# Cross-attention in plain float32: one product per term in the last attention block of a four-block decoder

## The reference, cut to what matters

```python
def _L3_xattn_ref(hidden_states, cross_attention_states, attention_mask, q_proj_w, k_proj_w, v_proj_w, o_proj_w, q_norm_w, k_norm_w):
    q = (hidden_states @ q_proj_w.T)...            # 32 heads of 128
    k = (cross_attention_states @ k_proj_w.T)...   # 8 kv heads, 64 keys per batch
    v = (cross_attention_states @ v_proj_w.T)...
    q = rmsnorm(q, q_norm_w); k = rmsnorm(k, k_norm_w)
    scores = einsum('bhqd,bhkd->bhqk', q, k) / sqrt(128) + attention_mask
    attn = softmax(scores)
    out = einsum('bhqk,bhkd->bhqd', attn, v)...
    return out @ o_proj_w.T
...
x = x + tanh(g_xattn[3]) * _L3_xattn_ref(_layernorm(x), ctx_4096, mask, ...)
```

## Time and profile before

| | us |
|---|---|
| median of 3 runs | 1882.77 |
| lowest, highest | 1882.39, 1884.41 |
| the profiled execution | 1874.59 |
| its span, first to last instruction | 1872.9 |

### The profile page before, as it was taken

How to read it: one execution, slowest core, us unless ns; L and a number is a source line. 1 busy time by engine, 2 the same in 40 slices (tenths; PEclk the granted TensorE clock), 3 DMA queues, 4 the chain that set the end, 5 groups by cost and what they waited for, 6 DMA issues and landing times.

```text
span 1872.9 us, 18291 instructions
## 1 busy us (share of the span) xinstructions
PE 1460.5 (78%) x6556; PEld 1020.8 (55%) x6556; DVE 1213.1 (65%) x1816; ACT 611.7 (33%) x912; POOL 348.9 (19%) x330
## 2 busy tenths in 40 slices
PE   7878778778746678578878888779999999997104
PEld 5545454445324545365746666557777777776101
DVE  4887888788885677542354444646666665667777
ACT  3544444444432233210121221134444344443003
POOL 1122132122213700010000000112212222123600
PEclk9998998989878799789569999989999999998556
DMA  5675776665572000002010112101101111000001
GB/s 193 156 181 137 143 178 150 160 141 138 117 136 99 34 11 1 0 23 68 0 34 17 46 38 77 48 9 57 57 23 39 53 57 57 1 1 1 0 0 45
DMA packets 37183, 127.69 MB, mean 68 GB/s; under 512 B 4288, under 2 KB 10304, under 8 KB 30896
## 3 DMA queue, kind: packets, MB, share of 16 engines
q1 hardware_dynamic: 26224, 83.38, 13.1%
q0 software_dynamic: 10880, 43.26, 13.0%
HBM read 72.63 MB, written 10.75 MB: 45 GB/s over the span
## 4 chain that ended last, share of the span: by engine, by line
PE 58%; DVE 20%; issue 10%; DVEq 5%; ACT 3%; POOL 1%; POOLq 1%; DMA 1%; SPq 0%
PE PS L151 10%; PE PS L153 9%; PE PS L152 9%; PE PS L492 6%; PE PS L467 4%; PE PS L825 3%; PE PS L861 3%; DVE AR L610 3%; DVE AR L2082 2%; DVEq L320 2%; DVE AR L631 2%; PE PS L451 2%; DVE AR L2076 2%; DVE AR L2080 1%; PE PS L847 1%
## 5 line engine op out<-in xcount | busy, mean ns | idle before, releaser
L492 PE MATMUL PS<-R,PT 128*128 128x512 f32 x256 | 158.0, 775 | 130.3 <-DVE X L646 130.3
L492 PEld LDWEIGHTS PS<-R,PT 128*128 128x128 f32 x256 | 61.5, 252 | 215.8 <-issue 215.8
L152 PE MATMUL PS<-R16r 128*128 128x512 f32 (+1 forms) x328 | 122.9, 375 | 0.0
L153 PE MATMUL PS<-R16r 128*128 128x512 f32 (+1 forms) x312 | 121.2, 388 | 0.0
L467 PE MATMUL PS<-R,HT 128*128 128x256 f32 x512 | 115.9, 379 | 0.0
L400 POOL DMA_DIRECT2D AR<-AR x40 | 49.6, 1240 | 307.7 <-DMA AR<-AR 239.4
L467 PEld LDWEIGHTS PS<-R,HT 128*128 128x128 f32 x512 | 94.8, 190 | 11.6
L151 PE MATMUL PS<-R16r,HTr 128*128 128x512 f32 (+1 forms) x224 | 91.3, 408 | 6.1 <-DVE X L1218 4.6
L151 PE MATMUL PS<-HTr,R16r 128*128 128x512 f32 (+1 forms) x240 | 90.4, 377 | 3.1 <-DVE R16r L193 1.6
L610 DVE SCALAR_TENSOR_TENSOR AR<-OT,AR 128x2112 f32<-128x2112 bf16 x32 | 75.5, 2359 | 21.8 <-ACT OT L555 19.4
L153 PE MATMUL PS<-HTr,R16r 128*128 128x512 f32 (+1 forms) x240 | 88.3, 368 | 0.0
(11 more groups left out here) (284 smaller groups left out, 3702.8 us busy)
## 6 DMA issues: line engine op xcount, KB each, us to landing
AR<-AR POOLq DMA_DIRECT2D x40, 1056.0 KB, 8.2
OR<-in_wo SPq DMA_DIRECT2D x12, 1024.0 KB, 5.0
dequantised<-AR SPq DMA_DIRECT2D x8, 1056.0 KB, 4.5
WR<-in_w0q SPq DMA_DIRECT2D x8, 1024.0 KB, 5.9
AR<-in_w3q SPq DMA_DIRECT2D x8, 1024.0 KB, 4.9
WR<-dequantised SPq DMA_DIRECT2D x22, 256.0 KB, 2.8
AR<-in_nf SPq DMA_DIRECT2D x4, 1056.0 KB, 6.0
nf_in<-in_nf SPq DMA_DIRECT2D x4, 1056.0 KB, 5.9
```

Of the source, the lines that this page charges most:

```text
L152: nc.tensor.matmul(out, ah, bl, start=False, stop=False)
L153: return nc.tensor.matmul(out, al, bh, start=False, stop=last_)
L492: i = nc.tensor.matmul(bank(5 + tt), PT[:, at:at + P], vo[:, pr, b, :], start=pr == 0, stop=pr == 1)
```

## The change

The queries and outputs of x3 are computed with one plain float32 product in the place of mm3, and nothing makes high and low parts for them any more. `VO`, `PT` and `HT0` are the float32 views of the same places. The rounds of `piece`, the folded pieces and the turned probabilities are released by ACT's copy alone. Query weights are loaded straight into one of two places that the product reads. `turn_p(u)`'s copies alternate between two halves of `PT`.

```diff
+        PLAIN = (0, 6, 7)
@@ dve_norm
             def low(t):
-                if n == 0:
+                if n in PLAIN:
                     return
@@ pe_norm
-                if t >= 2:
+                if t >= 2 and n in PLAIN:
+                    pe.wait_ge(hi_ready, T * n + t - 1)
+                elif t >= 2:
                     pe.wait_ge(lo_ready, T * (n - 1) + t - 1)
@@ act_norm
-                nc.scalar.copy((HT0 if n in (0, 7) else HTh)[:, :, t * P:(t + 1) * P],
+                nc.scalar.copy((HT0 if n in PLAIN else HTh)[:, :, t * P:(t + 1) * P],
@@ places
+        VO = R16[:, 4096:8192].rearrange("p (r b n) -> p r b n", r=2, b=B)
         def wq3(g):
+            at = 2048 if g % 2 else 7168
+            return AR[:, at:at + C * WQ].rearrange("p (c n) -> p c n", c=C)
+        def pt3(u):
+            return PT[:, (u % 2) * 512:(u % 2 + 1) * 512]
@@ sp_x3
             def load_q(g):
-                if g:
-                    sp.wait_ge(A3["q_split"], C * g)
-                sp.dma_start(WQ3, w3q_d[g]).then_inc(A3["q_in"], 16)
+                if g >= 2:
+                    sp.wait_ge(A3["q_mm"], 2 * B * (g - 1))
+                sp.dma_start(wq3(g).rearrange("p c n -> p (c n)"), w3q_d[g])\
+                    .then_inc(A3["q_in_odd" if g % 2 else "q_in"], 16)
...
             load_o(0)
+            load_q(1)
...
             for g in range(1, NG):
-                load_q(g)
                 load_kv(g)
                 if g + 1 < NG:
                     load_o(g + 1)
+                    load_q(g + 1)
@@ pool_x3: split_q and its calls go
-            split_q(0, range(C))
             pool_norm(pool, 6)
...
-                if g + 1 < NG:
-                    if b < 2:
-                        split_q(g + 1, (2 * b, 2 * b + 1))
-                    if b == 1:
-                        key_scale(g + 1)
+                if g + 1 < NG and b == 1:
+                    key_scale(g + 1)
@@ pe_x3
             def piece(r):
                 if r:
-                    if (r - 1) % PIECES3 in (0, 3):
-                        pe.wait_ge(A3["piece_hi"], r)
-                    else:
-                        pe.wait_ge(A3["piece_lo"], folded(r - 1) + 1)
+                    pe.wait_ge(A3["piece_sb"], r)
@@ queries
                 for c in range(C):
-                    if b == 0 and tt == 0:
-                        pe.wait_ge(A3["q_split"], C * g + c + 1)
-                    i = mm3(bank(tt), HTh[:, c, tok], HTl[:, c, tok], hi[:, c], lo[:, c], c == 0, c == C - 1)
+                    i = nc.tensor.matmul(bank(tt), HT0[:, c, tok], wq3(g)[:, c], start=c == 0, stop=c == C - 1)
@@ turn_p, outputs
-                    pe.wait_ge(A3["pt_lo"], u)
+                    pe.wait_ge(A3["pt_ready"], u)
...
-                    pe.wait_ge(A3["pt_lo"], u + 1)
-                    pe.wait_ge(A3["piece_lo"], 8 * g + 2 * b + 2)
+                    pe.wait_ge(A3["pt_ready"], u + 1)
+                    pe.wait_ge(A3["piece_sb"], PIECES3 * g + VO_AT[b] + 2)
...
-                    i = mm3(bank(5 + tt), PTh[:, at:at + P], PTl[:, at:at + P], VOh[:, pr, b, :], VOl[:, pr, b, :],
-                            pr == 0, pr == 1)
+                    i = nc.tensor.matmul(bank(5 + tt), pt3(u)[:, at:at + P], VO[:, pr, b, :], start=pr == 0, stop=pr == 1)
@@ act_x3: high_q and its calls go; folded_high becomes
+            def folded(g, b, pr):
                 act.wait_ge(A3["piece_mm"], PIECES3 * g + VO_AT[b] + pr + 1)
-                nc.scalar.copy(VOh[:, pr, b, :], bank(7)).then_inc(A3["piece_hi"], 1)
+                nc.scalar.copy(VO[:, pr, b, :], bank(7)).then_inc(A3["piece_sb"], 1)
@@ dve_x3: probs_low and folded_low go, with all their calls
```

More of the change, by code:

```diff
@@ L135, in build @@
                         "nf_in nf_in_odd nf_v nf_mask nf_acc nf_rise nf_summed nf_free nf_out nf_stored nf_used")
-        A3 = Sems("a3", "kv_in q_in o_in o_in_odd mask_in q_hi q_split piece_mm piece_hi piece_lo ksq krs kn_ready q_mm q_copy "
-                        "q_sq sq_sum qrs tq_mm qT_ready s_mm s_read shifted exps probs t_mm pt_hi pt_lo out_mm acc")
+        A3 = Sems("a3", "kv_in q_in q_in_odd o_in o_in_odd mask_in piece_mm piece_sb ksq krs kn_ready q_mm q_copy "
+                        "q_sq sq_sum qrs tq_mm qT_ready s_mm s_read shifted exps probs t_mm pt_ready out_mm acc")
         F0 = Sems("f0", "w_in packed w_hi split mm acc")
@@ L694, in build @@
         VO_AT = (1, 4, 6, 8)
-        X3B = ARr[:, 0:4096]
         Q_ROW = AR[:, 4096:5120]
@@ L698, in build @@
         QT3 = AR[:, 6144:7168]
-        WQ3 = AR[:, 7168:9216]
         WKV3 = AR[:, 9216:10240]
@@ L821, in fold_outputs @@
                     pe.wait_ge(A3["o_in_odd" if g % 2 else "o_in"], 16 * (g // 2 + 1))
-                    pe.wait_ge(A3["piece_hi"], PIECES3 * g + 1)
+                    pe.wait_ge(A3["piece_sb"], PIECES3 * g + 1)
                 for hh in range(2):
@@ L833, in queries @@
                 tok = slice((2 * b + tt) * P, (2 * b + tt + 1) * P)
-                hi, lo = wq3(g)
+                if b == 0 and tt == 0:
+                    pe.wait_ge(A3["q_in_odd" if g % 2 else "q_in"], 16 * (g // 2 + 1))
                 for c in range(C):
-                    if b == 0 and tt == 0:
-                        pe.wait_ge(A3["q_split"], C * g + c + 1)
-                    i = mm3(bank(tt), HTh[:, c, tok], HTl[:, c, tok], hi[:, c], lo[:, c], c == 0, c == C - 1)
+                    i = nc.tensor.matmul(bank(tt), HT0[:, c, tok], wq3(g)[:, c], start=c == 0, stop=c == C - 1)
                 i.then_inc(A3["q_mm"], 1)
@@ L853, in scores @@
                 if b == 0:
-                    pe.wait_ge(A3["piece_hi"], PIECES3 * g + 4)
+                    pe.wait_ge(A3["piece_sb"], PIECES3 * g + 4)
                 if u:
@@ L939, in act_x3 @@
         def act_x3(act):
[L940 to L944, removed]
             def keys_values(g):
                 act.wait_ge(A3["piece_mm"], PIECES3 * g + 1)
-                nc.scalar.copy(kvs[:], bank(7 if g else 3)).then_inc(A3["piece_hi"], 1)
+                nc.scalar.copy(kvs[:], bank(7 if g else 3)).then_inc(A3["piece_sb"], 1)
             def keys(g):
@@ L952, in keys @@
                 nc.scalar.activation(kT[:], bank(7)[:, 0:B * SK], ACT.Copy, scale=qkw[:, 0:1])\
-                    .then_inc(A3["piece_hi"], 1)
-            def folded_high(g, b, pr):
+                    .then_inc(A3["piece_sb"], 1)
+            def folded(g, b, pr):
                 act.wait_ge(A3["piece_mm"], PIECES3 * g + VO_AT[b] + pr + 1)
-                nc.scalar.copy(VOh[:, pr, b, :], bank(7)).then_inc(A3["piece_hi"], 1)
+                nc.scalar.copy(VO[:, pr, b, :], bank(7)).then_inc(A3["piece_sb"], 1)
             def query_row(u, tt):
@@ L977, in probs_t @@
                 act.wait_ge(A3["t_mm"], u + 1)
-                nc.scalar.copy(PTh, bank(4)).then_inc(A3["pt_hi"], 1)
-            high_q(0, range(C))
+                nc.scalar.copy(pt3(u), bank(4)).then_inc(A3["pt_ready"], 1)
             keys_values(0)
@@ L992, in act_x3 @@
             act_norm(act, 6, range(6, 8))
-            folded_high(0, 0, 0)
-            folded_high(0, 0, 1)
+            folded(0, 0, 0)
+            folded(0, 0, 1)
             query_square(1, 0)
@@ L998, in act_x3 @@
             query_turned(1, 0)
-            folded_high(0, 1, 0)
+            folded(0, 1, 0)
             query_turned(1, 1)
-            folded_high(0, 1, 1)
+            folded(0, 1, 1)
             exps(0)
-            folded_high(0, 2, 0)
-            folded_high(0, 2, 1)
+            folded(0, 2, 0)
+            folded(0, 2, 1)
             for u in range(NU0):
@@ L1021, in act_x3 @@
                 if vg < NG:
-                    folded_high(vg, vb, 0)
+                    folded(vg, vb, 0)
                 if more:
@@ L1025, in act_x3 @@
                     query_turned(u + 2, 1)
-                if b < 2 and g + 1 < NG:
-                    high_q(g + 1, (2 * b, 2 * b + 1))
                 if vg < NG:
-                    folded_high(vg, vb, 1)
+                    folded(vg, vb, 1)
                 if b == 0 and g + 1 < NG:
@@ L1037, in key_squares @@
             def key_squares(g):
-                dve.wait_ge(A3["piece_hi"], PIECES3 * g + 1)
+                dve.wait_ge(A3["piece_sb"], PIECES3 * g + 1)
                 nc.vector.tensor_tensor(Q_SQ3, kvs[:, 0:2 * DH], kvs[:, 0:2 * DH], ALU.mult)
@@ L1078, in norm @@
                 softmax_norm(dve, s_slot(u), 8, SK, stat_slot(2, u)).then_inc(A3["probs"], 1)
[L1080 to L1087, removed]
             def add(u, tt):
@@ L1098, in dve_x3 @@
             square_sum(0, 1)
-            folded_low(0, 0, 0)
-            folded_low(0, 0, 1)
             key_norm(0)
@@ L1112, in dve_x3 @@
                 more = u + 2 < NU0
-                vg, vb = divmod(u - 1 + B, B)
                 if u + 1 < NU0:
                     shift(u + 1)
-                probs_low(u)
                 if more:
@@ L1126, in dve_x3 @@
                     key_squares(g + 1)
```

(4 more changed lines are left out.)

16 lines of the change are left out of this document (removed).

## The result

The kernel after takes 1926.77 us (median of 4 runs, 1925.71 to 1929.26), the kernel before 1882.58 (4 runs, 1879.59 to 1884.41): by the ratio estimated over the runs 1.0238 times as long, 95% interval 1.022 to 1.0256 (the two medians give 1.0235). It was forecast at 1923.3 us, +40.5; measured is +44.2.

The account below looks back on a forecast made before the run. PE's unbroken stream was taken to bound x3: 49.5 (30 units) - 6 (start) - 2 (end) - 1 (group edges) = +40.5 us on 1882.8, giving 1923.3 us; main case 1913 to 1931, widened to 1909 to 1936.

Parts of the forecast that it names:

- What bounds x3: Middle of x3: PE streams without a stall, so the stage lasts the sum of PE's products; work spared elsewhere is worth nothing.
- a rhythm of DVE and ACT: Rival in x3: DVE and ACT set the unit, which shortens by 2.07 us; 1816 us, faster; chance 0.04.
- The price of a plain product: On PE in x3: a plain float32 product costs 0.86 us against 0.70 for the three fp32r products it replaces.
- estimate of 0.65 us for three fp32r products: Skill's pass rule for PE: three fp32r passes 0.65 us, loss 0.21 us a term; rows had 0.70 and decided.
- The unit: One x3 unit on PE: +1.60 to +1.70, taken as +1.65, from 13.83 to 15.48 us.
- I let this go with the change of type: Edges of x3's fp32r blocks: some 0.09 us late after the first product, booked as vanishing with plain float32.
- 384 terms: Cross-check over x3's replaced products: 0.16 us lost per term by the rows, some 60 us in all.
- The start: Start of x3, where PE waits for DVE's low parts and the keys' norm: -8 to -4 us, taken as -6.
- the case that the prediction held open: Start of x3: `scores(0)` at 1.2 GHz again after PE waited, giving back 3 to 4 of the 8 us.
- The end: End of x3, where `outputs(30)` waited 3.85 us for `probs_low`: -1 to -3 us, taken as -2.
- F3 behind it is a chain of small DVE steps and only shifts: Behind the end of x3: F3 moves in time only; no change in its length was booked.
- 49.5 - 1: Middle of x3: 30 units at +1.65 give +49.5 us; edges at the groups, under 1 us either way, taken as -1.

Follow-up runs that it names:

- half_chunks: The kernel after, with queries summed over two of the four feature chunks; one profile: a unit of 12.38 us, the 30 units 101.3 us shorter.
- o_only: The kernel before with only outputs in plain float32, without low parts of folded values and probabilities, queries left as three fp32r products; ratio 1.0093.
- high_only: The kernel before with only the high*high product of each three in x3's queries and outputs, low parts still made and waited for; 1760.1 us, one profile.
- filler: The kernel after plus 24 identity transposes ahead of norm 7's turn of tile 6; one profile: 1935.28 us, F3's first transpose 44.7 us after `turn_p(30)`.
- edge_filler: The kernel before with plain outputs only in units 0, 1, 2, 30, 31, plus 24 identity transposes before norm 7's tile 6 turn; 1875.58 us, ratio 0.9962.

## Why the prediction was right, and where it was not

*What bounds x3.* Right, and shown from four sides: PE is busy for 438.00 of 438.00 us in the kernel after; with 8 records of 0.429 us (3.43 us) taken out of a unit, the unit is 3.44 us shorter (half_chunks); the two halves of the change add up (57.8 of 58.0); and with all of DVE's subtractions gone the stage still grows by what the dearer products add (o_only). The rival, a rhythm of DVE and ACT, needed the kernel before to be held at 13.83 us a unit by it; with the same work on DVE and fewer products, high_only has units of 9.3 to 11.8 us.

*The price of a plain product.* Right: 8 records in 3.43 to 3.49 us, 0.86 us a product, as read in the first attention block. An fp32r product takes 0.232 us on average in the middle of x3 (0.233 was taken), 0.695 for three. The estimate of 0.86 us that the prediction worked out from the four passes of the Trainium skill (FP8 and Floating Point Precision, "TensorE Precision Notes") agrees with the plain product. Its estimate of 0.65 us for three fp32r products does not, and it was rightly left out of the sum.

*The unit: +1.65 forecast, +1.99 measured.* This is the term that was mis-sized. The step that failed is "I let this go with the change of type": some 0.09 us in each of the four fp32r blocks of a unit were counted as a cost that goes. None of it goes, 4 x 0.085 = 0.34 us a unit. Two of the four blocks stand behind transposes. There the late second product stood behind an early first one, nothing in the balance. I had looked at the distance behind the first product and not at the one in front of it, which stands in the same rows: four transposes take 0.35 us ahead of an fp32r product (1426.22 to 1426.57) and 0.53 ahead of a float32 one (1429.41 to 1429.93), 0.09 of which is the edge towards 64 columns. The other two stand behind scores and behind a fold. There the edge is real and the plain block has it too: `queries` behind scores take 3.49 us, where those behind transposes take 3.43, with 0.03 more in front of them; `outputs` behind a fold take 1.82, where four records of 0.429 make 1.72. Without edges the sum was to be had from prices that the prediction states itself: 12 terms a unit, each 0.86 for 0.70, or by the finer figures 12 x (0.858 - 0.695) = 1.96 us. Its 384 terms and "some 60" us were nearer than its sum by blocks. Over the 30 units the loss is 58.0 us and not 30 x 1.99, since those with keys, values or turned keys grew by 1.9 to 2.0.

*The start: -6 forecast, -4.8 measured.* Right in place and size; o_only, with -5.9, shows that it comes with the low parts of the outputs' half. The clock was at 1.2 GHz for `scores(0)` again (3.65 us for 16 records), the case that the prediction held open.

*The end: -2 forecast, +3.0 measured.* The first part was right and larger (the first logits come 12.3 us after `turn_p(30)` and not 16.3). A wait of 1.81 us for norm 7 and then the clock took it back; with the clock held up the end is -1.0 (filler). "F3 behind it is a chain of small DVE steps and only shifts" is the sentence that failed: the logits are PE's, and what they cost depends on where the clock's fall lands.

*The total.* 1923.3 against 1926.8 looks better than it was. By the traces at an equal first stage the change is +54.5, where +40.5 was summed: 9.5 us too little in the middle (58.0, where 49.5 - 1 stood), 5.0 at the end and 1.2 at the start, less the 1.7 us that the stretches outside x3 gained and no term had. That the total came out 3.5 us from the forecast is luck: the timed runs of before happened to lie 5 to 10 us above its profile and those of after within 3 us of theirs, which the traces put down to x0 and not to the change.

## What to carry to other kernels

Where one engine streams without a stall, count its time in distances between starts, and price the new instruction from the nearest block that already uses it; here plain float32 cost 0.86 us where three fp32r products cost 0.70, and what other engines were spared was worth nothing in the 30 streaming units and some 5 us at the start, where PE had waited for them. When a block goes, look at the distances on both sides of it, and at the block that takes its place, before an edge is booked as a saving. A removed wait may move a fall of the TensorE clock onto the work behind it, so the end of a stage needs its own check.

## What the runs showed of the hardware

- A plain float32 product of 128x128 weights and 512 columns is two records 0.429 us apart at 2.4 GHz; an fp32r one is one record, 0.232 us. Its weights loaded in 190 ns, those of fp32r in 188.
- An fp32r product behind float32 transposes starts 0.08 to 0.09 us earlier than a plain one (0.35 us for four transposes and not 0.44), and its successor 0.08 to 0.09 us late: at that edge the two types come out even.
- 2.65 us of transposes without a use, in place of a 1.81 us wait, kept the granted clock at 2.4 GHz over the 32 logits behind them (3.65 us and not 6.86, one trace; 4.15 in edge_filler).
- One stage that nothing touched ended between 570.1 and 583.2 us from run to run; totals alone tell +44 (timed) or +52 (profiled) for a change that costs +54.5 at an equal x0.
